# Aggregations of per-sample weights interleaved with the first convolutions, and the two load queues starting on opposite halves

## The reference

```python
# layer 0: grouped convolution, 4 groups, 9 taps, padding 4, plus a constant for each sample and channel
x = x + conv(x, weight) + (c @ c_weight.T)[:, :, None] + bias[None, :, None]
# layer 1: a 1x1 convolution whose weights are mixed for each sample from 8 experts
h = gelu(c @ W0 + b0); h = gelu(h @ W1 + b1)
att = softmax(h @ W2 + b2)                       # (128, 8)
agg_w = einsum('bk,koi->boi', att, weight)       # (128, 64, 64)
x = x + einsum('boi,bih->boh', agg_w, x) + (att @ bias_k)[:, :, None]
```

## Time and profile before

| | before |
|---|---|
| median of 3 runs | 261.31 us (260.1 to 261.76) |
| profiled execution, its own time | 261.07 us |
| its span in the profile | 258.6 us |
| TensorE busy | 241.1 us, 93% |
| VectorE busy | 225.9 us, 87% |
| ScalarE busy | 88.1 us, 34% |
| GpSimd busy | 25.1 us, 10% |
| bytes moved by DMA | 68.77 MB, mean 266 GB/s |

### The profile page before, as it was taken

How to read it: one execution, slowest core, us unless ns; L and a number is a source line. 1 busy time by engine, 2 the same in 40 slices (tenths; PEclk the granted TensorE clock), 3 DMA queues, 4 the chain that set the end, 5 groups by cost and what they waited for, 6 DMA issues and landing times.

```text
span 258.6 us, 5721 instructions
## 1 busy us (share of the span) xinstructions
PE 241.1 (93%) x2144; PEld 112.5 (44%) x2144; DVE 225.9 (87%) x146; ACT 88.1 (34%) x142; POOL 25.1 (10%) x48
## 2 busy tenths in 40 slices
PE   2579989999999999999999999999999999999980
PEld 1322323344444444444444455555555555554520
DVE  1350599999999999999999999999999999999871
ACT  2352301233333334241414333333334142333091
POOL 0010152010101001010101010100101010101000
PEclk9999999999999999999999999999999999999998
DMA  7999619999999999999999999999999998544078
GB/s 229 313 253 207 146 38 223 272 214 313 278 260 344 227 381 249 369 252 331 298 314 285 294 325 290 330 250 370 261 361 246 329 301 294 215 162 165 0 309 340
DMA packets 29337, 68.77 MB, mean 266 GB/s; under 512 B 3264, under 2 KB 5312, under 8 KB 29328
## 3 DMA queue, kind: packets, MB, share of 16 engines
q1 hardware_dynamic: 19392, 51.31, 63.0%
q10 hardware_dynamic: 9936, 17.34, 28.5%
HBM read 35.08 MB, written 33.55 MB: 265 GB/s over the span
## 4 chain that ended last, share of the span: by engine, by line
PE 80%; issue 7%; DVE 6%; ACT 2%; DMA 2%; ACTq 0%; POOLq 0%; DVEq 0%; POOL 0%
PE yps L475 56%; PE zps L495 18%; PE zps L458 3%; DVE ycol L372 2%; DVE xph L364 2%; DMA mlps<-in_mlp 2%; DVE ynat L381 1%; ACT mixt L291 1%; PE zps L522 1%; PE yps L522 1%; ACT zout L283 1%; ACT L312 0%; PE zps L562 0%; POOLq L44 0%; ACTq L306 0%
## 5 line engine op out<-in xcount | busy, mean ns | idle before, releaser
L475 PE MATMUL yps<-xph,wraw 64*64 64x512 f32 x1488 | 169.9, 595 | 1.3 <-DVE xph L364 1.1
L283 ACT ACTIVATE zout<-zps,gamu 128x512 f32<-128x512 f32 x120 | 72.8, 688 | 136.6 <-PE zps L495 117.0
L475 PEld LDWEIGHTS yps<-xph,wraw 64*64 64x64 f32 x1488 | 76.7, 133 | 88.5 <-issue 88.4
L372 DVE STREAM_TRANSPOSE ycol<-yps 128x1024 f32<-128x1024 f32 x62 | 75.7, 1227 | 13.7 <-PE yps L475 12.6
L364 DVE STREAM_TRANSPOSE xph<-xin 128x2112 f32<-128x2112 f32 x32 | 74.7, 2337 | 0.0
L381 DVE STREAM_TRANSPOSE ynat<-ycol 128x2048 f32<-128x2048 f32 x30 | 67.6, 2290 | 1.1
L495 PE MATMUL zps<-ynat,mixv 64*64 64x512 f32 x480 | 61.4, 609 | 0.7 <-ACT zout L283 0.6
L495 PEld LDWEIGHTS zps<-ynat,mixv 64*64 64x64 f32 x480 | 24.6, 132 | 28.8 <-issue 28.7
L228 POOL COPY mixv<-mixt 128x512 f32 (+1 forms) x16 | 17.6, 1099 | 176.9 <-ACT zout L283 176.9
L291 ACT ACTIVATE mixt<-zps 128x1024 f32<-128x1024 f32 x8 | 7.8, 1021 | 11.7 <-PE zps L458 11.7
L458 PE MATMUL zps<-zout 32*128 32x512 f32 x32 | 9.2, 1011 | 2.2 <-ACT mixt L291 1.3
(11 more groups left out here) (47 smaller groups left out, 30.4 us busy)
## 6 DMA issues: line engine op xcount, KB each, us to landing
out<-zout SPq DMA_DIRECT2D x60, 512.0 KB, 9.6
xin<-in_x SPq DMA_DIRECT2D x60, 258.0 KB, 9.1
xin<-in_x ACTq DMA_DIRECT2D x60, 258.0 KB, 8.5
out<-xin SPq DMA_DIRECT2D x4, 512.0 KB, 4.3
xin<-in_x ACTq DMA_DIRECT2D x4, 132.0 KB, 5.8
xin<-in_x SPq DMA_DIRECT2D x4, 130.0 KB, 5.8
xin<-in_x SPq DMA_DIRECT2D x4, 128.0 KB, 6.2
xin<-in_x ACTq DMA_DIRECT2D x4, 126.0 KB, 6.2
```

The source lines that it names most:

```text
L283: nc.scalar.activation(zout[:, o].rearrange("p (i c j q) -> p c i j q", i=2, c=2, q=PH)[:, c], zps[:, at:at + BANK].rearrange("p (q i j) - ...
L372: nc.vector.transpose(ycol[:, :, :, :, :, g].rearrange("p i s j q c -> p i (s j) q c"), yps[:, 2 * BANK * (g % 2):2 * BANK * (g % 2) + 2 * ...
L475: last = nc.tensor.matmul(yps[C * c:C * c + C, at:at + BANK].rearrange("p (s f) -> p s f", s=S // 2), wsum[rows, b, g], xph[slot][c][rows, ...
```

## The change

TensorE's hand-written order at the start is changed: only the first aggregation stands ahead of the first convolution, and the other three stand one each behind convolutions 0, 1 and 2 of step 0. The constants matmul moves behind all four convolutions of step 0. ScalarE issues its part of load 2 behind the fourth gather copy and not behind the eighth. In each load, ScalarE's queue asks for the second half of the length first; SP's queue still asks for the first half first.

```diff
@@ scalar: load(u, slot) @@
-                for i in range(2):
+                for i in (1, 0):
                     for t in range(2):
                         act.dma_start(*x_piece(slot, u, i, 1, t)).then_inc(x_in[slot], 16)
@@ scalar @@
             for a in range(CH):
                 gather(a, 0)
                 gather(a, 1)
-            load(2, 0)
+                if a == 1:
+                    load(2, 0)
             act.wait_ge(const_mm, 1)
@@ tensor @@
             aggregate(0)
-            aggregate(1)
-            aggregate(2)
             pe.wait_ge(w_sum, 1)
             conv(0, 0, 0)
+            aggregate(1)
+            conv(0, 0, 1)
+            aggregate(2)
+            conv(0, 0, 2)
             aggregate(3)
-            conv(0, 0, 1)
+            conv(0, 0, 3)
             pe.wait_ge(agg_out, 2 * CH)
             pe.wait_ge(const_eye, 1)
             nc.tensor.matmul(gps, beta[:], consts, start=True, stop=True).then_inc(const_mm, 1)
-            conv(0, 0, 2)
-            conv(0, 0, 3)
             conv(1, 1, 0)
             pe.wait_ge(const_out, 1)
             pe.wait_ge(const_sum, 6)
```

## The result

| | before | changed |
|---|---|---|
| median, 20 runs each | 261.01 us | 258.86 us (257.78 to 260.33) |
| ratio changed to before | | 0.9931 (95% interval 0.991 to 0.9951) |
| profiled execution, its own time | 261.07 us | 258.55 us |
| its span | 258.6 us | 256.7 us |

The change takes 0.7% off, 1.8 us by the ratio, against the 2.1 us forecast: clear of the noise by its interval, and within the 1% that the prediction counted as no change. The profiled executions differ by 2.5 us, of which 1.9 is span. In the changed kernel the lines of `aggregate`, `conv` and `mix` are one further down (L459, L476, L496).

The account below looks back on a forecast made before the run. TensorE was taken to set the pace, with recoverable idle time at the start: 3.64 us earlier, cut to 2.0 by a wait of 1.6, plus 0.1, gives 261.07 - 2.1 = 259.0 us. The range was 257.4 to 262.0.

Parts of the forecast that it names:

- VectorE's two long transposes end: VectorE's step 0 transposes behind column transpose 3: end at 38.3 against 42.78, 4.4 us ahead, so the mix doesn't wait.
- gain behind the start: Whole time kept to the end: 2.0 us from TensorE's start plus 0.1 from a later stand, 2.1 us.
- the new wait: TensorE ahead of the constants reduction: one convolution of 2.78 us covers a 4.37 us chain, so it stands 1.6 us.
- The stand at 47.54: TensorE's stand of 0.13 us ahead of the steady loop: should go as well, worth 0.1 us.
- The start and the order: TensorE's start: first convolution at 16.35 against 21.20, and that of step 1 at 33.61 against 37.25.
- the 3.64: First convolution of step 1: starts 3.64 us earlier, 33.61 against 37.25, before the reduction's wait takes part of it.
- ScalarE and load 2: ScalarE's four DMA issues between gathers 1 and 2: 2.5 us, ending about 24.8, ahead of the gather wanted at 25.96; no cost.
- The halves: Order of halves in ScalarE's loads: no engine waits for loads, so 0 us, with a small chance for a loss.
- (1): Rival at the first convolutions: clock rises late, 3.1 us lost (262.1) to 9.2 us (268); chance 0.17.
- (2): Rival: clock rises within the first 2 us of convolution 0, up to 2 us less, 257.0 to 258.0; chance 0.12.
- (3): Rival: no wait appears ahead of the constants reduction, so 3.64 and 0.1 us remain, 257.3; chance 0.05.
- (4): Rival: late gathers or issue on ScalarE, or reordered loads holding up VectorE, take the gain back; 260.3 to 262; chance 0.07.

Follow-up runs that it names:

- e3: Changed kernel with the constants reduction moved behind convolution (1, 1); 257.25 us, ratio 0.9835 to the kernel before.
- e11: Repeat, on another chip, of the changed kernel with the constants reduction behind convolution (1, 1); 257.90 us, ratio 0.988 to the kernel before.
- e5: Changed kernel with one extra unused GpSimd product at the head of the constants chain; 260.64 us, ratio 0.9975 to the kernel before.
- e6: Kernel before with one extra unused GpSimd product at the head of the constants chain; 260.6 us, ratio 0.9996.
- e1: Kernel before with only ScalarE's loads starting on the second half; 261.39 us, ratio 1.0005.
- e2: Changed kernel with ScalarE's loads back on the first half first; 259.76 us, ratio 0.9939 to the kernel before.
- e4: Changed kernel with aggregation 1 back ahead of the first convolution; 260.35 us, ratio 0.9946 to the kernel before.
- e9: Changed kernel with ScalarE's part of load 2 back behind all gathers; 259.58 us, ratio 0.9952 to the kernel before.
- e10: Changed kernel run again without edits, on another chip; 258.34 us, ratio 0.9901 to the kernel before.
- e7: Changed kernel with two unused matmuls in TensorE's wait for the constants reduction; 259.58 us, ratio 0.995 to the kernel before.
- e8: Changed kernel with the reduction behind convolution (1, 1) and an unused matmul ahead of the first convolution; 256.38 us, ratio 0.9838 to the kernel before.
- e12: Repeat of the kernel with the reduction behind convolution (1, 1) and a filler matmul ahead of the first convolution; 256.87 us, ratio 0.9827 to the kernel before.

## Why the prediction was right

| step of the prediction | forecast | changed kernel |
|---|---|---|
| first convolution starts | 16.35 | 16.37 |
| it takes | 4.73 | 5.03 |
| first convolution of step 1 starts | 33.61 | 33.90 |
| GpSimd is through with the constants | 37.98 | 38.26 |
| convolution (1, 1) starts | 38.4 | 38.80 |
| VectorE's two long transposes end | 38.3 | 38.69 |
| first mix starts | 41.1 | 41.54 |
| gain behind the start | 2.1 | 1.98 (252.48 to 250.50 for the last instruction of VectorE) |

The mechanism is the one forecast; that the gain comes within 0.12 us of the forecast is in part luck. At convolution (1, 1) the changed kernel is 1.63 us ahead (40.43 to 38.80) and not 2.0, because the first convolution ran longer and the new wait is longer. The stand at 47.54, put at 0.1, gave back 0.35: the two convolutions around it take 5.16 us and not 5.52.

**The start and the order** held to 0.4 us, and nearly all of the 0.3 to 0.4 is the first convolution, where the clock rose later: its weight loads stand 0.86 us apart (18.10, 18.96, 19.81) as those in the earlier trace rows did, and the last of its six groups is the only one that is shorter.

**The new wait** was forecast at 1.6 us and is 1.77 in the trace. That it is the term which took nearly half of the 3.64 is shown three ways: the reduction moved gives 1.96 us in the traces (e3, e11), the chain lengthened costs about its full length (e5), and the same in the kernel before costs nothing (e6). Whoever had stopped at the first convolution of step 1 would have forecast 257.3.

**ScalarE and load 2.** The issue ran from 22.62 to 25.15 and the next copy at 26.34, so it was hidden as worked out:

```profile
22.62 1.24 ACTq L273 DMA_DIRECT2D xin<-in_x  x2
...
26.34 1.94 ACT L291 ACTIVATE mixt<-zps 128x1024 f32<-128x1024 f32 x2 [1.87 <-PE zps L459]
```

**The halves** were put at 0, and e1 (ratio 1.0005) and e2 (0.9939 against 0.9931) show nothing else.

**The rivals.** (1), the late rise, did not happen in the sense meant: after one aggregation the clock was up in all profiles with the new order (in e2 the rise came inside that aggregation, which took 1.38 us and not 1.07). The rival was also priced too low. I had taken a convolution at the lower level at 2.0 us more, 4.73 less 2.74, but the 4.73 already has the rise in it. In e2 and e11 it took 5.40, and twice 2.74 is 5.5. A rise at the end of convolution 1 would so have cost about 4.5 us (1.06 for the aggregation, 2.7 for that convolution, 0.7 for the first), an estimate from these rows, and not 3.1. And I had looked for the clock's risk at the first convolution only. The wait that I had priced at its own length has one too: of six profiles of kernels with TensorE idle ahead of the reduction (changed, e2, e4, e5, e9, e10) three show the clock at 0.50 behind it, for 1.7 us each; of the eight without such idle time there (before, e1, e3, e6, e7, e8, e11, e12) none does. The Trainium skill (TensorE: Matmul & The Clock Gate, Part 1: The HAM clock gate) says that the clock falls back when TensorE goes idle and that activity releases it; the traces agree as to the direction, with 1.78 us of idle time in e2. The same idle time does not always do it: 1.77 us in the changed kernel's own profile and 1.78 in e10's left the clock up, as did 1.15 us ahead of 37.25 in the kernel before. How often it happens over the changed kernel's 20 runs is not shown, but the record bounds it. A fall such as e2's lowers the mean granted clock of an execution by 0.0066, and every profile shows the clock at 0.50 again in its last microseconds, which lowers it by 0.002 (e10) to 0.010 (e7). So only runs of 0.991 or less can have had a fall. There are five, and they are the five slowest, 259.68 to 260.33 us; the other fifteen took 257.78 to 259.14. That fits a fall in about a quarter of the runs. It is no proof, since e7's profiled execution has 0.990 without a fall. (2), the early rise, did not happen in this profile; its moment varies from run to run (below). (3) is refuted by the wait of 1.77 us and by e5. (4) is refuted by the traces, apart from what e9 leaves open.

## What to carry to other kernels

When work moves forward on the engine that binds, ask what the moved instructions had covered: here three convolutions had hidden a chain of 4.4 us on two other engines, and the new order left one. Move the consumer of that chain back as well (e3: ratio 0.9835 and 0.988 against 0.9931), and price a new wait on TensorE at its length plus a fall of the clock that can follow it (1.7 us here, in three of six profiles). A faster transfer is worth looking at only where an engine waits for one.

## What the runs showed of the hardware that was not expected

**The first convolution's length is spread over 2 us from run to run.** It begins at the lower clock each time and has the same instructions, and took 3.42, 4.18, 4.21, 4.31, 4.31, 4.73, 4.75, 5.03, 5.17, 5.22, 5.40 and 5.40 us in twelve profiles (e1, e6, e5, e3, e10, before, e12, changed, e7, e9, e2, e11; 3.42 also in e8). What ran ahead of it may matter, but doesn't order these numbers: with three aggregations ahead it took 3.42, 4.18 and 4.73, with one aggregation and a filler 3.42 and 4.75, and with one aggregation and idle time 4.21 to 5.40 in eight profiles, five of them above 5.0. That TensorE's idle time ahead of the first convolution delays the rise, on average by part of a microsecond, is suggested by this and by the medians of e8 and e12, and not shown. The last four stores land in 4.3 us in some executions and 5.4 to 5.6 in others (e1, e3, e4, e7, e12); all five of those have the halves swapped, but six others with the halves swapped have 4.3. These two account for much of the difference between the profiled executions (the changed kernel's and e10's, of one kernel, differ by 0.71 us in time and 0.72 in the first convolution), and are as large as the effect under study.

**Two queues on opposite halves.** In e1 the landing times fell as shown above (9.6 to 5.5 us for stores), though the DMA engines moved the same bytes: 303 GB/s in 98 to 112 us against 307. In the stretch from 20 to 26 us, where only loads are under way, the rate stayed at 209 GB/s, against 207 before. The Trainium skill (SBUF — State Buffer, "Can I just issue two DMAs to hit both halves?") answers no, two such transfers serialize. The rate of the loads, 209 against 207 GB/s, agrees with it. It doesn't account for the landing times in the steady loop; why they fall is open.
